# First loop of a fused two-layer decoder: weight loads in six groups spread over the loop, folded context weights, small counts in bf16

## The reference, cut to what matters

```
x = layernorm(x + attn(x))          # 16 heads of 8; softmax(q k / sqrt(8)) v; splat flow, gated
x = layernorm(x + xattn(x, ctx))    # query i sees only context row i (i < 64); every other query sees all rows alike
#   xattn out = attn @ (c @ Wv.T + bv) @ Wo.T + bo
# splats: d2 = |x|^2 + |s|^2 - 2 x s ; infl = exp(-d2 / 2 scale^2) |importance| ; flow = infl @ decode(...)
thr = sort(|W|)[k - 1], sort(|W|)[n - k]   # for W1, W2, b1, b2 of the experts
```

## Time and profile before

| what | value |
|---|---|
| median of 3 runs | 2076.66 us (2075.89 to 2093.12) |
| the profiled execution's own time | 2077.49 us |
| its span, first to last instruction | 2075.7 us |
| SP issues its first weight transfer | at 2.02 us |
| granted TensorE clock, mean share of full speed | 0.901 |
| PE, DVE, ACT, POOL busy | 84%, 66%, 58%, 50% of the span |

### The profile page before, as it was taken

The page is one execution under the profiler, slowest core; times in us unless marked ns, Lnnn a source line. Parts: engine busy times, 40 slices in busy tenths (PEclk is TensorE's granted clock), DMA queues, the critical chain, the costliest instruction groups (busy, mean ns, idle before and its releaser), DMA issues. The chain is left out here.

```text
span 2075.7 us, 43022 instructions
## 1 busy us (share of the span) xinstructions
PE 1748.0 (84%) x15192; PEld 1332.2 (64%) x15192; DVE 1378.3 (66%) x4612; ACT 1208.6 (58%) x2909; POOL 1035.6 (50%) x1578
## 2 busy tenths in 40 slices
PE   3999989998588999999999999999838999569940
PEld 1666666665476777777777777777625666459940
DVE  3677776774567777777778877788656887441127
ACT  1465555554378777776776777776414777234412
POOL 0456565654334556655555556566522332245365
PEclk9799898998799999999999999999968999669975
DMA  4000000000300000000000000000000000055322
GB/s 56 6 9 14 15 14 8 15 11 8 90 1 1 2 1 6 8 7 7 2 6 8 6 8 7 5 4 5 4 27 8 23 27 20 27 112 79 65 61 81
DMA packets 70108, 44.76 MB, mean 22 GB/s; under 512 B 26432, under 2 KB 62410, under 8 KB 69706
## 3 DMA queue, kind: packets, MB, share of 16 engines
q1 hardware_dynamic: 55256, 29.79, 5.3%
q0 software_dynamic: 4608, 9.45, 3.1%
q10 hardware_dynamic: 10034, 2.77, 0.7%
HBM read 27.31 MB, written 14.16 MB: 20 GB/s over the span
## 5 line engine op out<-in xcount | busy, mean ns | idle before, releaser
L2133 POOL TENSOR_SCALAR probs<-probs,rsums 128x128 f32<-128x128 f32 (+1 forms) x512 | 208.3, 425 | 328.9 <-DVE rsums L2030 328.8
L946 POOL TENSOR_SCALAR at_least<-magnitudes,candidates 128x512 bf16<-128x512 f32 x128 | 198.0, 1563 | 211.0 <-DVE candidates L842 211.0
L2014 DVE CUSTOM_DVE_ANT_0 probs<-dist,pq,nmin 128x128 f32<-128x128 f32 (+1 forms) x512 | 181.3, 410 | 121.4 <-PE pq L1497 121.0
L1762 ACT ACTIVATE probs<-probs,low 128x130 f32<-128x130 f32 (+1 forms) x512 | 227.7, 462 | 6.1 <-DVE low L2014 5.9
L913 DVE TENSOR_REDUCE negmax<-ps_scores 128x4 f32<-128x1024 f32 x128 | 156.5, 1223 | 102.3 <-PE ps_scores L573 100.8
L731 ACT ACTIVATE pT<-ps_scoresT 128x1024 f32<-128x1024 f32 x128 | 131.2, 1025 | 77.7 <-PE ps_scoresT L582 70.2
L2024 DVE COPY pT<-pq 128x384 f32<-128x384 f32 x256 | 130.2, 550 | 5.2 <-PE pq L1512 5.2
L1675 ACT ACTIVATE qn<-pq 128x512 f32<-128x512 f32 x128 | 77.1, 602 | 81.7 <-PE pq L1354 80.1
L1497 PE MATMUL pq<-k1T,q1T 64*128 64x128 f32 (+1 forms) x1024 | 119.2, 351 | 1.9 <-DVE low L2014 1.4
L3115 POOL DMA_INDIRECT m_x<-token_rows,m_idx_put x80 | 75.7, 946 | 80.0 <-DVE m_idx_put L3045 32.8
L3067 DVE COPY m_y<-pm 128x256 f32<-128x256 f32 x40 | 17.0, 425 | 140.3 <-PE pm L2953 140.3
(11 more groups left out here) (531 smaller groups left out, 5371.6 us busy)
## 6 DMA issues: line engine op xcount, KB each, us to landing
expert_answers<-m_y SPq DMA_DIRECT2D x40, 128.0 KB, 2.0
m_w<-in_L_ffn_moe_w_dram SPq DMA_DIRECT2D x16, 256.0 KB, 5.8
x<-in_x_dram SPq DMA_DIRECT2D x16, 128.0 KB, 2.1
x_mid<-x SPq DMA_DIRECT2D x16, 128.0 KB, 1.9
y<-x_mid SPq DMA_DIRECT2D x16, 128.0 KB, 2.2
x_mid<-y SPq DMA_DIRECT2D x16, 128.0 KB, 1.8
cx<-x_mid SPq DMA_DIRECT2D x8, 256.0 KB, 3.2
token_rows<-c_hn SPq DMA_DIRECT2D x8, 256.0 KB, 2.0
```

The source lines that it names most:

```text
L946: pool.tensor_scalar(at_least[:, a, :], mags[:, 512 * (a // 2):512 * (a // 2) + 512], cf[:, a:a + 1], None, ALU.is_ge).then_inc(mask_ready ...
L1762: ins = act.activation(probs[:, a, keys_nulls(i, w)], probs[:, a, keys_nulls(i, w)], ACT.Exp, bias=low[:, a, i:i + 1], scale=-1.0, accum_o ...
L2014: ins = dve.tensor_tensor_reduce(probs[:, a + t, keys(i, w)], dist[:, (1 - t) * P:N], ps[:, t * P:t * P + w], slopes[h], nmin[u][:, t, h:h ...
L2133: ins = pool.tensor_scalar(probs[:, a + t, keys(i, w)], probs[:, a + t, keys(i, w)], rsums[:, a + t, i:i + 1], 1.0, ALU.mult, ALU.mult)
```

## The change

The common preparation goes. Loads are in six groups with a semaphore each; SP issues most of them between the loads of the first three sequences, ACT the Wk and splat ones. Wq and Wk come plain and DVE spreads them on chip. What was prepared before the loop becomes stages that run for u = 0 alone: `splats` (step -7), `gate_bias` (-2), `magnitudes` (0), `turn_out` (11), `fold_cross` (16). POOL fills v, enc and trans. `cross_values` goes: PE multiplies Wv and Wo once in `fold_cross`, with the biases, and `cross_out` takes `cT` directly; the mean column of `cT` becomes 128 columns and `cT` has six sets. The small counts are compared into bf16 and multiplied with `ones_bf`.

```diff
-        vx = sets(4, "vx", [P, N])
+        cT = sets(6, "cT", [P, S_CTX + P])
-            (-10, "project_x"), (-1, "vg"), (1, "cross_values"), (3, "influence_tm"), (6, "encode"),
+            (-10, "project_x"), (-1, "vg"), (3, "influence_tm"), (6, "encode"),
...
+            (-7, "splats"), (-2, "gate_bias"), (0, "magnitudes"), (11, "turn_out"),
@@ tensor @@
-            pe.wait_ge(loaded, 16 * len(loads))
...
-            pe.wait_ge(setup_done, 3)
+            def splats(u):
+                if u:
+                    return
+                pe.wait_ge(splat_loaded, 16 * len(splat_loads))
+                pe.transpose(ps[:, 0:NS], sp_raw[:], ident[0:NS, 0:NS]).then_inc(ring.filled("spT"), 1)
+            def turn_out(u):
+                if u:
+                    return
+                pe.transpose(ps[:, 0:P], wo_raw[:], ident[:])
+                pe.transpose(ps[0:64, P:P + NS], bt_raw[:], ident[0:NS, 0:NS]).then_inc(ring.filled("woT"), 1)
+            def fold_cross(u):
+                if u:
+                    return
+                pe.matmul(ps[:, 0:D], wv_raw[:], wo_x[:], start=True, stop=True)
+                pe.matmul(ps[0:3, D:2 * D], bv_x[:], wo_x[:], start=True, stop=True).then_inc(ring.filled("w_x"), 1)
-            def cross_values(u):
...
-                pe.matmul(ps[:, 256:272], ones_sq[:], at_least_small[:].rearrange("p a n -> p (a n)"),
+                pe.matmul(ps[:, 256:272], ones_bf[:], at_least_small[:].rearrange("p a n -> p (a n)"),
@@ cross_out @@
-                    pe.matmul(ps[:, t * D:(t + 1) * D], vx[u][:, t * P:(t + 1) * P], wo_x[:], start=True, stop=False)
+                    pe.matmul(ps[:, t * D:(t + 1) * D], cT[u][:, t * S_CTX:t * S_CTX + P], w_x[:], start=True, stop=False)
@@ scalar @@
-            for dst, src in loads[1::2]:
+            act.dma_start(*qk_loads[1]).then_inc(qk_loaded, 16)
+            for dst, src in splat_loads:
...
-                act.activation(cT[u][:, S_CTX:S_CTX + 1], csum[u][:], ACT.Copy, scale=1.0 / S_CTX)\
+                act.activation(cT[u][:, S_CTX:], csum[u][:].to_broadcast([P, P]), ACT.Copy, scale=1.0 / S_CTX)\
-            def cross_values(u):
@@ vector @@
+            dve.wait_ge(qk_loaded, 16 * len(qk_loads))
+            for i in range(3):
+                ins = dve.tensor_scalar(wq[:, :, :, DH0 * i:DH0 * (i + 1)], wq_raw[:].rearrange(heads, g=GROUPS, j=4),
+                                        DH0 ** -0.5, None, ALU.mult)
+            for i in range(3):
+                ins = dve.tensor_copy(wk[:, :, :, DH0 * i:DH0 * (i + 1)], wk_raw[:].rearrange(heads, g=GROUPS, j=4))
...
+            def fold_cross(u):
+                dve.wait_ge(w_x_ready, 1)
+                link(dve.tensor_tensor(bo_x[:], bo_x[:], ps[0:3, D:2 * D], ALU.add))
+                three_parts(dve, link, bo_x3, bo_x, bo_work, pick)
@@ sync @@
-            for dst, src in loads[0::2]:
+            sp_eng.dma_start(*qk_loads[0]).then_inc(qk_loaded, 16)
...
+                    if u == 0:
+                        for dst, src in vg_loads:
+                    if u == 1:
+                        for dst, src in ffn_loads:
+                        for dst, src in flow_loads:
+                    if u == 2:
+                        for dst, src in out_loads:
```

More of the change, by code:

```diff
@@ L379, in loop_1 @@
         first, last = sems[n_setup].num, sems[-1].num
[L381 to L386, removed]
+        heads = "k (g j d) -> k g j d"
+        qk_loads = [(wq_raw[:], A["L0_attn_Wq"]), (wk_raw[:], A["L0_attn_Wk"])]
+        splat_loads = [
+            (sp_raw[:], A["L0_attn_splat_positions"]),
+            (scl[:, 0:1], col(A["L0_attn_splat_scales"])), (imp[:, 0:1], col(A["L0_attn_splat_importance"])),
+        ]
+        vg_loads = [(wv[:], A["L0_attn_Wv"]), (wg[:], A["L0_attn_Wg"]), (bg[:, 0:1], col(A["L0_attn_bg"]))]
+        ffn_loads = [
+            (K["w1"][:], A["L0_ffn_W1"]), (K["w2"][:], A["L0_ffn_W2"].rearrange("(c p) n -> p c n", p=P)),
+            (K["b1"][:], A["L0_ffn_b1"].rearrange("(c p) -> p c", p=P)), (K["b2c"][:], col(A["L0_ffn_b2"])),
+        ]
+        flow_loads = [
             (we[:], A["L0_attn_We"]), (be[0:64, :], col(A["L0_attn_be"])), (be[64:128, :], col(A["L0_attn_be"])),
@@ L408, in loop_1 @@
         stages = [
-            (8, "max_rows"), (24, "mixed"), (27, "project_out"), (31, "cross_out"), (22, "normalise"),
+            (8, "max_rows"), (24, "mixed"), (27, "project_out"), (16, "fold_cross"), (31, "cross_out"), (22, "normalise"),
             (5, "decide0"), (9, "decide1"), (1, "candidates0"), (5, "candidates1"),
@@ L441, in project_qk @@
                     ring.wait_read(pe, "xT", u)
+                if u == 0 and half == 0:
+                    pe.wait_ge(wq_ready if name == "q" else wk_ready, 1)
                 ps = ring.open(pe, name, u, half, held=0.95)
@@ L454, in distances @@
             def distances(u):
+                if u == 0:
+                    ring.wait_read(pe, "spT")
+                    pe.wait_ge(ones_ready, 1)
                 ps = ring.open(pe, "d2", u, held=1.6)
@@ L743, in _ @@
                          influence_tm=influence_tm, gather=gather, encode=encode, decode=decode, turn_rows=max_rows,
-                         cross_values=cross_values)
+                         fold_cross=fold_cross, splats=splats, turn_out=turn_out)
             with act.Fori(0, B // U) as it:
@@ L815, in split_qk, with fold_cross @@
                                          ALU.mult, ALU.add).then_inc(ring.read(name, u, half), 1)
+            def fold_cross(u):
+                if u:
+                    return
+                ps = ring.wait(dve, "w_x")
+                dve.wait_ge(w_x_ready, 1)
+                link(dve.tensor_tensor(bo_x[:], bo_x[:], ps[0:3, D:2 * D], ALU.add))
+                dve.sem_inc(ring.read("w_x"), 1)
+                three_parts(dve, link, bo_x3, bo_x, bo_work, pick)
+                dve.sem_inc(parts_ready, 1)
             def distances(u):
@@ L921, in _ @@
                          influence=influence, read_transform=transform, read_flow=flow, max_rows=max_rows,
-                         normalise=normalise, mixed=mix, project_out=lambda u: norm_stats(u, "y", 0),
+                         normalise=normalise, mixed=mix, fold_cross=fold_cross, splats=splats, gate_bias=gate_bias,
+                         magnitudes=magnitudes, turn_out=turn_out, project_out=lambda u: norm_stats(u, "y", 0),
                          cross_out=lambda u: norm_stats(u, "yx", 1))
```

201 lines of the change are left out of this document (126 added, 75 removed).

## The result

The changed kernel took 2069.64 us (median of 20 runs, 2052.78 to 2079.08) beside 2075.97 us for the kernel before (20 runs): a ratio of 0.9956, interval 0.9936 to 0.9976. Two more sets of runs gave 0.9939 [0.9919, 0.9959] and 0.9919 [0.9896, 0.9942]. So the change gains 6 to 15 us where 33 were forecast. The forecast of 2044 us and the whole range up to 2056 missed it, and so did the 0.88 on "faster": the result lies within 1%.

The account below looks back on a forecast made before the run. PE's own work was taken to bound the first loop (busy 92% from 90 to 490 us), after 30 us nearly idle. Gains 25.6 + 6.7 + 3.6 less 3.2 made 32.7 us, so 2044 us; 8-in-10 range 2034 to 2056.

Parts of the forecast that it names:

- Part 1, the way in: Start to first scores: PE starts at 5.5 us, first scores at 20.7 instead of 46.28, 25.6 us gained.
- other estimate, 4.2: PE's start by the Trainium skill's DMA rule, total 1.3 us lower; not used, because the row measured 3.4 us.
- It does not start early: Rival at the start: first load group late, PE starts at 15 us instead of 5.5; 2053 us, chance 0.06.
- Part 2, the one-off work: Magnitudes, turn_out and fold_cross, now inside the first loop, lose 3.2 us together; bounds 1.0 and 4.5.
- Part 3, each sequence: First loop: bf16 small counts gain 6.7 us, dropping the cross values matmul 3.6 us.
- its rival bound: First loop, small count: gain of only 2 us if PE merely waits longer for negmax.
- only the way in counts: Rival: PE work removed from the loop becomes waits for negmax and placed maxima; gain 22.4, 2054 us, chance 0.14.
- Banks: First loop: encode's bank wait of 1.2 us unchanged; one head product waits 0 to 0.3 us, 8 times.
- The sum: Whole kernel: 25.6 + 6.7 + 3.6 - 3.2 = 32.7 us gained, median 2044 us.
- the clock loses: Rival, loop from 90 us on: more half-clock steps at 2.2 us each; 26 more give 2101 us; chance 0.03.
- The clock gains too: Rival: clock rises to 90 us, about 7 us, as much again if later dips shrink; 2033 us, chance 0.08.

Follow-up runs that it names:

- before_again: The kernel before, unaltered, profiled a second time: 2077.46 us (one run).
- d_work_back: The changed kernel with f32 small counts and a context product with two ACT copies put back per sequence: 2070.2 us, ratio 0.9963 to the kernel before.
- dw_wide: The changed kernel with that loop work put back and transform products reading up to 32 columns instead of 4: 2056.73 us, ratio 0.989 to the kernel before.
- bw_wide: The kernel before with only its transform products reading up to 32 columns instead of 4: 2070.21 us, ratio 0.9956.
- w_again: The changed kernel with transform products reading up to 32 columns instead of 4, run again: 2042.81 us, ratio 0.9796 to the kernel before (4 runs).
- after_again: The changed kernel, unaltered, profiled a second time: 2063.61 us, ratio 0.9939 to the kernel before.
- b_idle: The kernel before with 48 small POOL clearings ahead of its first load, first scores 9.4 us later: 2101.47 us, ratio 1.011.
- eb_wide: The kernel before with bf16 small counts and transform products reading up to 32 columns instead of 4: ratio 0.9932.

## Why the prediction was wrong

**Part 1, the way in: right, and some 2 us too small.** PE turned x at 4.36 us, at the lower bound of 4.4, not at 5.5: the context was issued at 1.75, not 2.1, and PE could start 2.6 us later, not 3.4. The prediction's other estimate, 4.2, was nearer than its row. From there to the first scores it took 14.0 us, not 15.2. Against the rows that the prediction started from (46.28) the stage gained 27.9, against before_again 26.8, where 25.6 were forecast. "It does not start early" is refuted.

**Part 2, the one-off work: too small.** The magnitudes were to cost 0.4 us; DVE ran them from 20.38 ahead of a `negmax` that began at 22.75, and PE waited 2.45 us for it. DVE's chain of `fold_cross` was to cost 1.3; at 72.17 PE has waited 1.77 us for the split that stood behind it. With PE's own products and transposes as forecast (1.5) that makes an estimated 5.7 us instead of 3.2, over the bound of 4.5. The whole part was never run alone: d_work_back and dw_wide, which keep it and have the loop's old work, take 10.4 and 8.0 us more in pairs and loop's end than before_again and bw_wide, but the clock of the loop's end is in that.

**Part 3, each sequence: right in size, with wide products.** The forecast was 6.7 + 3.6 = 10.3 us; dw_wide against w_again shows 10.3 between profiles (that the two agree to the tenth is luck, as single profiles go), and the wide small count alone showed 3.8 of its 6.7, its rival bound being 2. Between d_work_back and after_again, at the lower clock, it was 7.9. Longer waits for `pT` and `negmax` did come, which I had not foreseen, because I placed the scores behind the cross values by `negmax` alone and did not look at ACT. They were nearly offset: from dw_wide to w_again these two grew by 5.8 and 4.2 us, but the waits for the placed maxima fell by 4.7, and all of PE's waits in the pairs grew only from 35.9 to 37.8. So "only the way in counts" is not what happened either.

**Banks: right.** `encode` waits for ACT's `xsqT` 11 times now, 13.2 us, where it had waited by turns for ACT and for DVE, 14.6 us together. The second wait, which the prediction left out when it named two large ones, is this line of the kernel before:

```profile
PE ps L482 <- DVEq L886: 7.4, 6, 1.2
```

**The sum: this is the step that failed.** It took every stage that the change does not touch, and the clock of the loop, to stay as they were. They did not. Against the forecast -32.7, the mean of three profiles is -10.6: the way in 1.2 to the good, pairs and loop's end +3.8 where -10.3 + 3.2 = -7.1 was forecast, 10.9 to the bad, and the untouched stages behind them +12.4, of which 14.1 in the two of the third part. If the forecast is split as dw_wide and w_again split it, 8.0 of the 10.3 in the pairs, the first loss is 1.5 us in the pairs and 9.4 at the loop's end. It is mostly a loss of clock, and in that it is like the rival "the clock loses", which I gave 0.03; but neither its place nor its mechanism is the one that I wrote. I put it on the steps from 90 us on, and the pairs have a mean clock of 0.86 to 0.87 with the change and 0.87 to 0.88 without; the fall is behind them, at the loop's end, where 0.78 became 0.56 to 0.70 and the same 324 or 325 instructions kept PE busy 36.3 to 43.7 us instead of 32.9. And my reason, that full-width f32 passes are taken out, is not enough: d_work_back has them and its loop's end is at 0.57. Part 2, too small by an estimated 2.5 us, is in the first loss too. The second loss was no rival of mine at all, and b_idle shows that it needs no edit: before and before_again entered the third part at full clock and left it at 0.74 to 0.81, and a shift of 9.4 us was enough to end that.

What sets the clock of the loop's end and of the third part stays open. At the loop's end an edit of the counts alone brings the fall (0.56), giving the f32 work back does not lift it (0.57), and a shift of the kernel before does not bring it (b_idle, 0.78). In the third part it is not the time alone at which the stage starts: bw_wide and eb_wide start it within 1 us of each other (1583.8 and 1584.4) and take 192.5 and 200.9. No experiment changed the third part itself. Single profiles of one kernel also differ there by 3.6 us, and at the loop's end by 5.8, so the split between the stages is less sure than the medians.

"The clock gains too" did not happen: by the medians there is no gain beyond the way in. (Its own sum, 2044 less two times 7, gives 2030, not 2033.) What the runs did find is that the step behind the thin products stands at half clock, and taking that away beats both kernels: 2042.81 us on the chip where the kernel before took 2080.67 and 0.978 of it on another. But the change alone did not do it.

## What to carry to other kernels

Before adding up savings on a busy TensorE, mark which stages run at full clock and which do not, the untouched ones too, and ask whether they would stay so; a stage that ran at 0.98 in one profile can gain almost nothing and lose 13 us. To price a saving, make it also in a variant whose clock holds. Before you blame an edit for a stage that it does not touch, shift the unedited kernel by a few us and see whether that does the same. And look for long runs of products with very few columns: reading more of what already lies there, at no added length, gave 10 us in the kernel before, as much as the whole change there, and 20 to 30 in the changed one.

## What the hardware showed that I had not expected

- Runs of the changed kernel spread over 26 us, and their time goes with the mean granted clock: over its 20 runs about 15 us for each 0.01 (correlation -0.89).
- With less TensorE work a kernel was slower: 7.0 us of matmul taken out, ratio 1.0036 [1.0013, 1.0059].
- 64 products of 4 columns and of 32 take the same time at full clock (3.89 and 3.90 us), and the step behind them ran at 0.50 to 0.65 after the first and at 1.00 after the second, behind seven transforms of every profile.
- 9.4 us of added idle time at the start cost 22.9 us in the medians.
- The spreading of weights in runs of 8 numbers on DVE took 0.75 us for each of three scalings beside POOL's fills, and 0.19 us for each of three plain copies after them.
